# A state-space layer on one core: neighbouring products on TensorE, one scan for two heads, chunk ends computed once

## The reference, cut to what matters

```python
# x: 8 sequences of 512 tokens, 128 channels; H=32 heads of P=64 channels, N=64 states, G=8 groups, conv width 4
proj = rmsnorm(layernorm(x)) @ in_proj_w             # z | x,B,C | dt
xBC  = silu(causal depthwise conv4(xBC) + conv_b)
dt   = softplus(dt_raw + dt_bias); dA = exp(-dt * exp(A_log))
def step(h, inp):                                    # for each token
    h = dA_t * h + (dt_t * x_t) outer B_t
    y_t = h . C_t
y = y + D * xs;  g = rmsnorm per group(y * silu(z)) * gate_norm_w
x = x + (layernorm(x) + g @ out_proj_w)              # then a small feed-forward layer with ternary weights
```

## Time and profile before

| | us |
|---|---|
| median of 3 runs | 1143.55 |
| the profiled execution, its own time | 1145.73 |
| its span, first to last instruction | 1143.9 |
| PE busy | 1033.2 (90%) |
| DVE busy | 1059.9 (93%) |
| ACT busy | 970.0 (85%) |
| POOL busy | 868.6 (76%) |

### The profile page before, as it was taken

The page is one execution under the profiler, slowest core; times in us unless marked ns, Lnnn a source line. Parts: engine busy times, 40 slices in busy tenths (PEclk is TensorE's granted clock), DMA queues, the critical chain, the costliest instruction groups (busy, mean ns, idle before and its releaser), DMA issues.

```text
span 1143.9 us, 26227 instructions
## 1 busy us (share of the span) xinstructions
PE 1033.2 (90%) x8912; PEld 732.0 (64%) x8912; DVE 1059.9 (93%) x2004; ACT 970.0 (85%) x2836; POOL 868.6 (76%) x596
## 2 busy tenths in 40 slices
PE   1724789999999999999999999999999999996797
PEld 1603566676666666676666666766666666664576
DVE  7597999999999999999999999999999999989474
ACT  2767898999999999999999999999999999984464
POOL 7300356888888888888888888888888888885765
PEclk9955899999999999999999999999999999997899
DMA  6320000000000000000000000000000000021001
GB/s 170 117 86 0 10 1 2 1 1 2 1 30 2 2 2 29 2 2 2 29 2 2 2 29 2 2 2 29 2 1 1 21 1 2 1 78 46 1 29 46
DMA packets 28084, 22.58 MB, mean 20 GB/s; under 512 B 11696, under 2 KB 22576, under 8 KB 27824
## 3 DMA queue, kind: packets, MB, share of 16 engines
q1 hardware_dynamic: 25136, 20.90, 5.9%
q10 hardware_dynamic: 2816, 0.02, 0.1%
HBM read 12.78 MB, written 8.13 MB: 18 GB/s over the span
## 4 chain that ended last, share of the span: by engine, by line
PE 77%; DVE 14%; issue 3%; POOL 2%; ACT 2%; DMA 0%; POOLq 0%; DVEq 0%; ACTq 0%
PE bank L1713 10%; PE bank L1695 10%; PE bank L1625 8%; PE bank L1727 8%; PE bank L1641 8%; PE bank L1626 6%; PE bank L1627 6%; PE bank L1681 5%; PE bank L1662 5%; DVE conv L1191 4%; PE bank L1766 3%; PE bank L1738 2%; DVE lm L1181 2%; PE bank L1555 1%; PE bank L1746 1%
## 5 line engine op out<-in xcount | busy, mean ns | idle before, releaser
L1191 DVE SCALAR_TENSOR_TENSOR conv<-bank,cw,conv 128x509 f32<-128x509 f32 (+2 forms) x576 | 421.7, 743 | 16.6 <-ACT conv L762 8.6
L636 POOL TENSOR_TENSOR lm<-lm,cbs 128x1024 f32<-128x1024 f32 x128 | 304.3, 2377 | 75.7 <-ACT xw L866 75.7
L1181 DVE TENSOR_TENSOR_SCAN lm<-bank,ident 128x512 f32<-128x512 f32 x256 | 298.7, 1210 | 0.7 <-PE bank L1641 0.6
L911 ACT ACTIVATE xdt<-bank,dt_all 128x64 f32<-128x64 f32 x1024 | 222.3, 329 | 37.2 <-PE bank L1662 37.2
L866 ACT ACTIVATE xw<-xdt,lm 128x64 f32<-128x64 f32 x768 | 199.3, 365 | 0.0
L644 POOL TENSOR_TENSOR ssum<-ssum,sq 128x512 f32<-128x512 f32 x96 | 123.1, 1283 | 93.0 <-ACT sq L926 92.8
L1625 PE MATMUL bank<-xn_hi,w_hi 128*128 128x512 f32 x320 | 166.1, 519 | 13.8 <-DVE conv L1191 13.1
L615 POOL TENSOR_TENSOR gated<-gated,gate 128x512 f32<-128x512 f32 x128 | 164.9, 1288 | 15.9 <-DVE gated L1238 14.5
L626 POOL TENSOR_TENSOR gated<-gated,rbs 128x512 f32<-128x512 f32 x120 | 153.8, 1282 | 0.0
L877 ACT ACTIVATE conv<-bank,cb_bias,cw 128x512 f32<-128x512 f32 x189 | 142.6, 781 | 11.5 <-PE bank L1627 7.3
L1713 PEld LDWEIGHTS bank<-lm,xdt 128*64 128x64 f32 x2048 | 110.3, 137 | 63.7 <-issue 63.7
(11 more groups left out here) (217 smaller groups left out, 1766.5 us busy)
## 6 DMA issues: line engine op xcount, KB each, us to landing
lm<-in_L_attn_in_proj_w SPq DMA_DIRECT2D x1, 2048.0 KB, 11.7
xn_scratch<-chan SPq DMA_DIRECT2D x4, 512.0 KB, 4.6
r_stage<-residual_scratch SPq DMA_DIRECT2D x8, 256.0 KB, 2.9
xn_stage<-xn_scratch SPq DMA_DIRECT2D x7, 256.0 KB, 3.2
x_scratch<-r_stage SPq DMA_DIRECT2D x7, 256.0 KB, 2.0
gate<-in_L_attn_hidden_states SPq DMA_DIRECT2D x2, 512.0 KB, 4.6
cdec<-in_L_attn_hidden_states SPq DMA_DIRECT2D x2, 512.0 KB, 7.1
w_out<-in_L_attn_out_proj_w SPq DMA_DIRECT2D x8, 128.0 KB, 3.3
```

What stands on the lines that cost most here:

```text
L636: gp.tensor_tensor(lm[:, mr, :, :], lm[:, mr, :, :], cbs[:, :, :], ALU.mult).then_inc(m_done, 1)
L911: act.activation(xdt[:, r, at:at + HP], misc_of("xt", n)[:, at:at + HP], ACT.Copy, scale=dt_h).then_inc(xdt_done, 1)
L1181: V.tensor_tensor_scan(lm[:, m % R, a, :], bc_bank[(3 * m + a) % 2][:, :], ident4[:, :], 0.0, ALU.mult, ALU.add).then_inc(scanned, 1)
L1191: V.scalar_tensor_tensor(out=conv[:, ci % 4, shift:S], in0=tile_bank(b, n, t)[:, 0:S - shift], scalar=cw[:, q, t, KW - 1 - shift:KW - shif ...
```

## The change

- The PE order in a slot: states, inner y and state part of y stand next to each other in every slot; the output product, the gate's tile and the row products move behind them (in r = 0 the rows, gate tile and transposes stand ahead of them). In r = 3 the convolution tile is now first, and in r = 1 the gate tile is last, behind the transposes of B and of the factor.
- Banks 2 and 3 become one tensor `decays` of 1024 columns. Head 0's row goes to the first half, head 1's row and then the prefix products to the second, and one scan of 1024 with an identity of 1024 columns serves both heads.
- `pend` (chunk ends) is made once for all slots and batches: 16 small products after slot 4 of the first batch, and one copy on DVE. The copy in each slot goes.
- The first state is copied on ACT (`first_state`), right after `weigh`, in r = 0 after `scale_x`.
- The factor's columns are expanded on POOL, right after the root.
- The output product has the gated tokens stationary (four pieces of 128) and w_out moving, so the result has tokens on partitions; `copy_output` and `last_output` go, and DVE adds the residual straight from bank 7 at the head of slot 15.
- `misc_plan` has `xt` ahead of `s` in every slot, and on DVE the taps and state steps have another order.

```diff
 def misc_plan():
-            if r < 2:
-                plan += [(n, "s", LAG_STATE, 0), (n, "xt", LAG_SSD, 0)]
-            else:
-                plan += [(n, "xt", LAG_SSD, 0), (n, "s", LAG_STATE, 0)]
+            plan += [(n, "xt", LAG_SSD, 0), (n, "s", LAG_STATE, 0)]
...
+        low = [pb(f"bank{i}", [P, S]) for i in range(2)]
+        decays = pb("decays", [P, 2 * S])
+        bank = low + [decays[:, S * i:S * i + S] for i in range(2)] + [pb(f"bank{i}", [P, S]) for i in range(4, 8)]
...
 POOL, root
                     gp.tensor_tensor(rtok[:, :], vtok[:, :], neghalf[:, 0:2 * CH], ALU.pow).then_inc(rstd_done, 1)
+                    after(gp, rstd_done, UNITS, bb, v)
+                    after(gp, rbc_ready, UNITS, bb, v - 1)
+                    gp.tensor_copy(rexp[:, :, :], rtok[:, :].unsqueeze(2).broadcast_to([P, 2 * CH, HP])).then_inc(rexp_done, 1)
...
 ACT
+                def first_state():
+                    bb, m = back(b, n, LAG_STATE)
+                    after(act, s_ready, SLOTS, bb, m)
+                    after(act, y_ready, SLOTS, bb, m - 2)
+                    act.activation(hpk[:, m % 2, 0, :], misc_of("s", n)[:, 0:NS], ACT.Copy).then_inc(hfirst, 1)
...
 DVE
-                    for a in range(2):
-                        after(dve, bc_ready, 3 * SLOTS, bb, 3 * m + a)
-                        V.tensor_tensor_scan(lm[:, m % R, a, :], bc_bank[(3 * m + a) % 2][:, :], ident4[:, :], 0.0,
-                                             ALU.mult, ALU.add).then_inc(scanned, 1)
+                    after(dve, bc_ready, 3 * SLOTS, bb, 3 * m + 1)
+                    V.tensor_tensor_scan(lm[:, m % R, :, :].rearrange("p a s -> p (a s)"), decays[:, :], ident4[:, :], 0.0,
+                                         ALU.mult, ALU.add).then_inc(scanned, 1)
...
-                    V.tensor_copy(pend[:, m % R, :].unsqueeze(2),
-                                  bc_bank[(3 * m + 2) % 2][:, :].rearrange("p (c i) -> p c i", c=CH)[:, :, P - 1:P]).then_inc(pend_done, 1)
...
 PE
-                pm, pk = divmod(i - 2, 3)
-                if pk < 2:
-                    after(pe, scanned, 2 * SLOTS, bb, 2 * pm + pk)
-                else:
-                    after(pe, cdec_done, SLOTS, bb, pm)
+                if k == 1:
+                    after(pe, cdec_done, SLOTS, bb, m - 1)
+                else:
+                    after(pe, scanned, SLOTS, bb, m - 1 if k == 0 else m)
...
-                    last = MM(out_bank[:, :], w_out[:, m, :], gated[:, (m // R) % 2, m % R, :], start=(m == 0), stop=(m == SLOTS - 1))
+                    for c in range(CH):
+                        tok = slice(P * c, P * c + P)
+                        last = MM(out_bank[:, tok], gated[:, (m // R) % 2, m % R, tok], w_out[:, m, :],
+                                  start=(m == 0 and c == 0), stop=(m == SLOTS - 1 and c == CH - 1))
...
+                if n == R:
+                    ends = pr_parts[:, :].rearrange("k (c i) -> k c i", i=P)[:, :, P - 1:P].rearrange("k c i -> k (c i)")
+                    for m in range(SLOTS):
+                        last = MM(out_bank[:, NCH * m:NCH * m + NCH], sel[:, m, HP:HP + P], ends, start=True, stop=True)
+                    last.then_inc(pend_ready, 1)
```

More of the change, by code:

```diff
@@ L996, in slot @@
                     scale_x()
+                    first_state()
                     square()
@@ L1002, in slot @@
                     weigh()
+                    first_state()
                     activate(0)
-                    if not (b == NB and n == 9):
-                        expand_root(b, n)
                     scale_x()
@@ L1298, in slot @@
                                     ALU.subtract).then_inc(lo_done, 1)
-                if n == XO_SLOT and back(b, n, SLOTS) is not None:
-                    bb, _ = back(b, n, SLOTS)
-                    after(dve, xo_ready, 1, bb, 0)
-                    dve.wait_ge(res_loaded, bb * 16 + 16)
-                    xs = r_stage[:, :, :]
-                    V.tensor_tensor(xs, misc_of("xo", n).rearrange("p (c d) -> p c d", d=DM), xs, ALU.add).then_inc(x1_done, 1)
             slot(0, 0)
@@ L1569, in misc_free @@
                     who = back(bb, pn, lag) if pkind != "xn" else following(bb)
-                    if who is not None:
+                    if who is not None and pkind != "unused":
                         break
@@ L1787, in next_input @@
                     transpose_xn(xn_stage, misc_of("xn", n))
-                def last_output():
-                    if n != XO_SLOT or back(b, n, SLOTS) is None:
-                        return
-                    bb, _ = back(b, n, SLOTS)
-                    after(pe, out_copied, 1, bb, 0)
-                    misc_free(b, n, "xo")
-                    for c in range(CH):
-                        last = TR(misc_of("xo", n)[:, P * c:P * c + P], ocm[:, P * c:P * c + P], ident)
-                    last.then_inc(xo_ready, 1)
                 if r == 0:
```

150 lines of the change are left out of this document (65 added, 85 removed).

## The result

The changed kernel takes 1181.49 us (median of 4 runs, 1179.86 to 1186.41); the kernel before, on the same chip, 1144.94 (4 runs, 1142.07 to 1146.34). The ratio is 1.033, its 95% interval 1.0291 to 1.0368: 36.5 us slower. I had said 1164, inside 1137 to 1188. The sign came as forecast, and so did most of the waits. The size is nearly twice what I had: 1181 lies outside the 1151 to 1176 that I gave my own mechanism, and inside the stated range only because that range also covered the rivals.

What follows compares the result with a forecast made beforehand. A loop of waits through PE, DVE and ACT was taken as the bound: 29.28 us against 28.87 a group, taken as +0.55 times 32 groups = 17.6, plus 2.5 at the start, giving 1164 us, range 1137 to 1188.

Steps and rivals of the forecast that it cites:

- the loop through ACT: Closed chain of waits over PE, DVE and ACT, one turn a group of four slots: 29.28 us against 28.87 before.
- 1 PE, r = 3, tap to `decay_c`: After r = 2's last tap, PE does tile, transposes, S, W, Y and the row until landed: 3.88 us.
- 2 DVE, rest of r = 3: DVE from `decay_c` in r = 3: two taps, two state steps and skip, 2.93 us.
- 3 DVE, r = 0: DVE's scan, three taps, `decay_c` and two dependent state steps in r = 0: 5.60 us.
- 4 PE, C times B to two tiles: PE's C times B, row and two tiles of r = 1, with a restart at each end: 2.96 us.
- 5 ACT, r = 1: ACT's second `convolve`, `weigh`, first state, silu and `scale_x` to its end: 4.56 us.
- 6 PE, transposes of B to the row: PE's two sets of four transposes, gate's tile and row landed, with restarts: 2.05 us.
- 7 DVE, r = 2: DVE's scan, taps, state steps and `decay_c` in r = 2, to the last tap's end: 7.30 us.
- the start: Between slots 4 and 5, DVE waits for 16 small products at 0.12 each plus a 0.6 copy: 2.5 us.
- Sums win: Rival: waits fall where the other side is ahead, PE's sum of 28.2 is the period: 1125 us, chance 0.14.
- Equal: Rival: restarts and dependent taps cost nothing, loop 28.7 equals the old sum: about 1144 us, chance 0.11.
- Further: Rival: r = 0 holds `skip` until Y, dearer first state and PE restarts, 30.3 a group: 1191 us, chance 0.14.

Runs made afterwards that it cites:

- e10: The changed kernel with DVE's one copy of all chunk ends a slot later: 1181.04 us in one run.
- e7: The changed kernel's operations with two scans of 512 and other orders on PE, DVE and ACT: 1125.32 us, ratio 0.9834 to the kernel before.
- e1: The changed kernel with the gate's tile and head 1's row ahead of the transposes of B in r = 1: 1183.06 us, a batch 118.70.
- e3: The changed kernel with both state steps ahead of `decay_c` on DVE in r = 0: 1176.56 us, a batch 117.76.
- e8: The orders of e7 with the joined scan of 1024 columns in place of two: 1137.86 us, ratio 0.995, a batch 113.97.

## Why the prediction was right, and where its size was off

**Right: that a loop ends the period and no engine's sum, and by 0.08 us which.** PE waits ahead of the tile of r = 3 and ahead of the transposes of B, ACT for the gate's tile; a batch of 119.0 lies at the top of the 117 to 119 that I gave. That the loop through ACT came out as the longest, and not the direct one, was luck: I never counted the direct one, and it is shorter by 0.06 to 0.08. The seven terms, by the timeline of after:

| step | forecast | measured |
|---|---|---|
| 1 PE, r = 3, tap to `decay_c` | 3.88 | 3.99 |
| 2 DVE, rest of r = 3 | 2.93 | 2.96 |
| 3 DVE, r = 0 | 5.60 | 5.59 |
| 4 PE, C times B to two tiles | 2.96 | 3.06 |
| 5 ACT, r = 1 | 4.56 | 4.46 |
| 6 PE, transposes of B to the row | 2.05 | 2.19 |
| 7 DVE, r = 2 | 7.30 | 7.32 |
| sum | 29.28 | 29.57 |

The measured terms are distances along one turn of the trace, so their sum is the period whichever way round one takes; what bears the forecast out is each term by itself. With the 0.3 that I allowed for PE's restarts my upper value was 29.6. The restarts themselves are small: 0.05 us behind a tap and behind `scale_x`, 0.15 ahead of C times B. The single errors are 0.14 at most: the first state costs ACT 0.10 (547.35 to 547.46), where I had 0.20; W costs 0.98 and Y 0.80, as taken.

**Mis-sized: what the loop was compared with.** I set the loop's 29.28 against 28.87, a quarter of a batch. But a batch holds work that comes once in 16 slots, and the loop doesn't. The four slots of before without it take 6.38 + 8.02 + 8.00 + 6.19 = 28.59; only two slots of a batch are longer, by 0.69 and 0.60, and one is shorter by 0.19. So the loss is 29.57 - 28.59 = 0.98 a group, where I had 0.55 (of this 0.41 from the sum, against 0.69 with the right base). A part comes back: before, the once-a-batch work cost 115.50 - 4 x 28.59 = 1.14 a batch, after 119.02 - 4 x 29.57 = 0.74, as some of it falls into waits. 3.92 - 0.40 = 3.5 a batch is what the trace shows. The bare slot by slot distances were in the trace of before; I took the average because it was at hand.

**Mis-sized: the start.** I had 2.5 us there and the trace has 1.3 + 8.6, of which 3.5 is the steady loss: 6.4. DVE's wait for the 16 products and its copy are its first part,

```profile
122.35 0.69 DVE L1441 COPY pend<-bank 128x512 f32<-128x512 f32 x1 [2.74 <-PE bank L1927]
```

2.74 + 0.61 = 3.35, just the growth of that slot (5.60 to 8.96). But e10 shows that this isn't the cause, only the place: take it away and 0.7 of it is gained. PE in these slots stands before the transposes of B, which wait for ACT:

```profile
129.26 1.11 PE L1726 MATMUL bank<-ident,chan 128*128 128x128 f32 x4 [3.04 <-ACT xdt L911]
```

ACT is no slower here than later (`scale_x` spans 1.71 us) but starts late, behind tiles of PE. PE runs partly at the lower clock, 1.2 GHz: these four transposes span 1.11 us, where they span 0.65 later. That the loop is the same as later with longer terms is my reading; no run shows it apart, and I never worked the loop out for the start. The clock adds to it: between 130 and 140 us the rows of before and of after are

```profile
130.00:140.00 10.00, 7.27 (x66) 4.75 (x63) 9.81 (x21) 9.77 (x35) 4.75 (x2) 1.00 0.00 0
```

```profile
130.00:140.00 10.00, 6.95 (x35) 4.53 (x34) 7.82 (x11) 7.96 (x26) 2.38 (x1) 0.84 0.00 0
```

a granted clock of 1.00 before and 0.84 after.

**The end.** Of the +4.8, 3.3 are the last batch at the loop's pace, which my 32 groups hold. The 1.4 left was no term of my sum, and where it comes from stays open: two kernels whose end part is the same code differ there by 3.4 (below). So of the 35.8 us about 28 are the loop (3.5 + 21.1 + 3.3), where I had 17.6, and 6.4 are the start, where I had 2.5.

**Sizes beside the loop.** The output product takes 0.81 (526.62 to 527.43), where I had named about 0.95, and 0.88 ahead of a row (534.34 to 535.22). The old form took 0.86 there,

```profile
514.22 1.02 PE L1695 MATMUL bank<-gated,w_out 128*128 128x512 f32 x2
515.08 0.38 PE L1641 MATMUL bank<-da_parts,sel 96*128 96x512 bf16 x1
```

so it is 0.02 dearer and not 0.12. The scan costs 2.20 and spans 2.29, as taken; but the pair before cost 2.25 from its start (503.25) to the next,

```profile
505.50 1.38 DVE L1191 SCALAR_TENSOR_TENSOR conv<-bank,cw,conv 128x511 f32<-128x511 f32 x2
```

and I had set its span of 2.33 against a start distance: joining them saves 0.05 a slot, not 0.13. The expansion on POOL, which I bounded by 1.28, has a mean of 0.61:

```profile
L653 POOL COPY rexp<-rtok 128x512 f32<-128x512 f32 x22 | 13.4, 610 | 1.4
```

PE's sum came to 27.7 or 27.8 where I had 28.2 or 28.3. Part of this is a term that I put at nothing, the way into Y. Before, a row stood ahead of Y and not W:

```profile
521.72 0.39 PE L1641 MATMUL bank<-pr_parts,sel 96*128 96x512 bf16 x1
521.94 0.38 PE L1641 MATMUL bank<-da_parts,sel 96*128 96x512 bf16 x1
```

A row ahead of a row costs 0.22 (521.72 to 521.94), a row ahead of Y 0.31 (to 522.25): 0.09 a slot, which the new order saves. In r = 0 it comes back, where a row stands ahead of S now (539.49 to 539.80), so about 0.3 a group is left. DVE's sum I added up wrong: 0.13 + 0.07 + 0.13 is 0.33 a slot and not 0.25. With the 0.05 that joining the scans saves in fact it is 0.25, so two errors cancel: DVE's sum fell by 0.4 a group (28.6 to 28.2), where I had 0.3. None of this moved the time, because no engine's sum was the period.

**The rule that I weighed** (the Trainium skill, TensorEngine Tiling (Array Packing), Key Properties: a change of tiling mode drains the array, a change of tile in one mode doesn't). From S to W the trace agrees: W starts 0.40 after S (531.02 to 531.42), 0.50 where a full-array product follows. From W to Y, where the rows are cut otherwise, W costs 0.98 and Y 0.80, against 1.03 and 0.80 ahead of full-array products. For this step the rows can't decide, since no W here is followed by products cut like itself. But I had read that nothing is saved by putting Y behind W, and that is wrong: W costs 0.05 less than ahead of a row, and the 0.09 on the way into Y are gone.

**The rivals.** "Sums win" (1125, 0.14) failed for this order, yet e7 shows that it was not far off as a statement about the operations: with orders that let the engines run side by side, the same operations, with two scans in place of one, give 1125. That the number is the same is partly chance, as the rival had the joined scan, a sum of 28.2 on PE and 2.5 us at the start, and in e7 DVE and PE are both full at 27.9 a group. "Equal" needed dependent taps and restarts to be free; the four taps of r = 2, with one dependent pair, take 2.74 (524.52 to 527.26), 0.14 more than 4 x 0.65, and the forecast had 0.13. "Further" (1191) had dearer restarts and a held `skip`; both are absent, and its total lies 10 above the measured one for reasons that did not happen.

One rival was missing: that a second loop, the direct one, lies just behind the first. It changes no forecast of the change itself, but every forecast of a cure. Taken one by one, e1 to e3 give 2.6 us a batch; together 3.4.

**Open.** What each new operation brings by itself in orders that suit it (only the joined scan was tried: e7 against e8), which of the moves in e7 count, how the 6.4 us of the start divide between the loop and the clock, and the 1.4 us behind the last scan.

## What to carry to other kernels

When a change reorders several engines at once, write down the closed loops, not only the engines' sums, and compare a loop with the bare period of the same stretch of before, not with an average that holds once-a-batch work. Look for the second loop too: with two nearly equal ones a wait can vanish from the profile whole and give back a quarter of itself. Joining two operations to save a fixed cost is dear where a consumer or producer used the point between them: 0.05 us saved each time, 12 us lost in all.
